# Moving small copies and jump terms of one edge pass from VectorE to ScalarE in a four-layer graph network

## What is computed

```
val = att_self[edge_row] + att_neigh[edge_col]
mx = jax.ops.segment_max(val, edge_row, num_segments=n)
val_exp = jnp.exp(val - mx[edge_row]) * edge_val[:, None]
denom = jnp.clip(jax.ops.segment_sum(val_exp, edge_row, num_segments=n), 1e-10)
msg = val_exp[:, :, None] * h_neigh[edge_col]
agg = jax.ops.segment_sum(msg, edge_row, num_segments=n) / denom[:, :, None]
```

## Time and profile before

| what | value |
|---|---|
| median of the runs | 6677.1 us (6671.12 to 6688.41) |
| span of the profiled execution | 7599.6 us |
| `sorted_pass` in it | about 2970 to 3411 us, 56 groups |
| VectorE busy, whole program | 4666.3 us (61%) |
| GpSimd busy | 4386.9 us (58%) |
| ScalarE busy | 1410.9 us (19%) |
| TensorE matmuls | 1283.1 us (17%) |

### The profile page before, as it was taken

How to read it: one execution, slowest core, us unless ns; L and a number is a source line. 1 busy time by engine, 2 the same in 40 slices (tenths; PEclk the granted TensorE clock), 3 DMA queues, 4 the chain that set the end, 5 groups by cost and what they waited for, 6 DMA issues and landing times. The chain is left out here.

```text
span 7599.6 us, 37104 instructions
## 1 busy us (share of the span) xinstructions
PE 1283.1 (17%) x8049; PEld 1112.1 (15%) x8049; DVE 4666.3 (61%) x9328; ACT 1410.9 (19%) x3648; POOL 4386.9 (58%) x4445
## 2 busy tenths in 40 slices
PE   7100000143443333333000000370000001000000
PEld 6100000033343333332000000250000001000000
DVE  7677777687676667996677777544443434433435
ACT  0122212220000002442000000262222211222223
POOL 1666566545565554005666666426777767777775
PEclk9555555555555555556555555585555555555555
DMA  9555445323333224773555555203333332333332
GB/s 347 179 181 185 164 161 171 120 85 103 101 109 103 95 98 157 296 268 91 176 179 174 180 179 181 85 20 93 106 99 101 101 90 66 111 102 101 97 100 80
DMA packets 338944, 1032.97 MB, mean 136 GB/s; under 512 B 100325, under 2 KB 163137, under 8 KB 331294
## 3 DMA queue, kind: packets, MB, share of 16 engines
q0 software_dynamic: 166752, 401.68, 18.9%
q1 hardware_dynamic: 116642, 342.34, 12.9%
q10 hardware_dynamic: 55324, 286.57, 10.1%
HBM read 602.97 MB, written 427.39 MB: 136 GB/s over the span
## 5 line engine op out<-in xcount | busy, mean ns | idle before, releaser
L708 POOL DMA_INDIRECT rows<-table,idx x3136 | 3091.7, 986 | 1446.0 <-issue 1022.3
L635 POOL DMA_INDIRECT by_src<-ebuf,place x784 | 767.8, 979 | 561.4 <-DVE place L1277 295.9
L1280 DVE SCALAR_TENSOR_TENSOR psA<-psA,cont,dstf 128x128 f32<-128x128 f32 (+1 forms) x2349 | 838.0, 357 | 291.2 <-remote 205.9
L1269 DVE TENSOR_TENSOR sc<-rows,ebuf 128x56 f32<-128x56 f32 x112 | 28.2, 252 | 1196.5 <-DMA rows<-table,idx 1196.5
L1280 DVE SCALAR_TENSOR_TENSOR sums<-sums,cont,psA 128x128 f32<-128x128 f32 (+1 forms) x1512 | 521.2, 345 | 225.0 <-remote 139.9
L934 PE MATMUL psA<-dstf,ones 128*128 128x512 f32 x10 | 9.9, 1113 | 3446.9 <-DVE dstf L2169 3446.9
L803 PE MATMUL psA<-attr,sums 128*128 128x49 f32 x1568 | 406.0, 403 | 747.4 <-DVE attr L1458 735.3
L803 PEld LDWEIGHTS psA<-attr,sums 128*128 128x128 f32 x1568 | 397.0, 326 | 761.1 <-DVE attr L1458 748.7
L934 PEld LDWEIGHTS psA<-dstf,ones 128*128 128x128 f32 x10 | 2.7, 318 | 3448.6 <-issue 3448.6
L2050 DVE TENSOR_TENSOR_SCAN psA<-rows,psA 128x1980 f32<-128x1980 f32 x112 | 480.0, 4286 | 3.9
L1211 ACT ACTIVATE psA<-df 128x60 f32<-128x60 f32 (+1 forms) x168 | 40.4, 241 | 2104.9 <-DVE df L1269 1120.4
(11 more groups left out here) (332 smaller groups left out, 5548.4 us busy)
## 6 DMA issues: line engine op xcount, KB each, us to landing
dstf<-spread_wide SPq DMA_DIRECT2D x168, 924.0 KB
states<-sums ACTq DMA_DIRECT2D x150, 952.0 KB, 3.7
rows<-by_src SPq DMA_DIRECT2D x55, 1035.0 KB, 5.1
states<-sums ACTq DMA_DIRECT2D x56, 1008.0 KB
spread_wide<-sums SPq DMA_DIRECT2D x56, 924.0 KB, 24.3
states<-sums ACTq DMA_DIRECT2D x56, 903.0 KB
rows<-table,idx POOLq DMA_INDIRECT x3136
msg<-low_rows SPq DMA_DIRECT2D x56, 448.0 KB
```

Source lines behind the costliest of these rows:

```text
L635: pool.indirect_dma_start(by_src[:, :], bass.IndirectOffsetOnAxis(ap=place[:, s, j:j + 1], axis=0), payload[:, s, j, :], None).then_inc(so ...
L708: pool.indirect_dma_start(rows[:, at:at + GW[ph]], None, table[ph][:, :], bass.IndirectOffsetOnAxis(ap=idx[:, s, j:j + 1], axis=0)).then_i ...
L1269: return dve.tensor_tensor(o_, a_, b_, op)
L1280: return dve.scalar_tensor_tensor(o_, a_, s_, b_, op0, op1)
```

## The change

The three copies and the jump terms are computed by ScalarE, and three things follow from that in the order of the work.

- ScalarE gets `costs(g + 1)`: jump terms, carried maxima and scores, three ACTIVATEs. In its stream they stand behind the DMA issue of group g - 1 and in front of `scale_tail(g)`. They wait for `flags_ready` and tell `costs_ready`, for which `max_so_far` waits on VectorE.
- ScalarE gets `keep_max(g + 1)`, one ACTIVATE behind `exponentials(g + 1)`, which tells `kept_max`; the DMA that saves the group waits for it.
- On VectorE `chain_flags` runs two groups ahead (so `cg` has three buffers) and stands between rows 10 and 11. `edge_bias(g)` moves from behind row 11 to behind row 9. `messages` waits for `pass_saved`, which `keep_max` did before.
- Before the first group, `chain_flags(1)` follows `chain_flags(0)`, ahead of the first scan.

The change to `holds` alters a count that phases 3 and 4 do not use.

```diff
-        cg = sb("cg", [P, 2, B])
+        cg = sb("cg", [P, 3, B])
...
+                def costs(g):
+
+                    act.wait_ge(flags_ready, g + 1)
+                    act.activation(hb(nf)[:, :, 1:B + 1], cg[:, g % 3, :].unsqueeze(1).to_broadcast([P, 4, B]), ACT.Copy, scale=BIG, bias=-BIG)
+                    act.activation(hb(sc)[:, :, 0], hb(mx)[:, :, B], ACT.Copy)
+                    act.activation(hb(sc)[:, :, 1:B + 1], srows[g % 3][:, 1:B + 1, ROW:ROW + 4].rearrange("p b h -> p h b"), ACT.Copy).then_inc(costs_ready, 1)
+
+                def keep_max(g):
+
+                    if g >= 3:
+                        act.wait_ge(pass_saved[g % 3], 16 * (g // 3))
+                    act.activation(ssums[g % 3].rearrange("p (b w) -> p b w", w=136)[:, :, ROW:ROW + 4].rearrange("p b h -> p h b"),
+                                   hb(mx)[:, :, 1:B + 1], ACT.Copy).then_inc(kept_max, 1)
...
+                costs(0)
                 exponentials(0)
+                keep_max(0)
                 for g in range(NG):
+                    if g < NG - 1:
+                        costs(g + 1)
                     scale_tail(g)
...
                     if g < NG - 1:
                         exponentials(g + 1)
+                        keep_max(g + 1)
+                    act.wait_ge(kept_max, g + 1)
                     act.wait_ge(sums_ready, NG + g + 1)
...
-                def chain_costs(g):
-
-                    fronted()
-                    front(ts(hb(nf)[:, :, 1:B + 1], cg[:, g % 2, :].unsqueeze(1).to_broadcast([P, H, B]), -1.0, ALU.add, BIG, ALU.mult))
...
                 def max_so_far(g):
 
-                    fronted()
+                    dve.wait_ge(costs_ready, g + 1)
...
-                    fronted()
+                    dve.wait_ge(flags_ready, g + 1)
                     dve.wait_ge(weighed, g + 1)
                     dve.wait_ge(sums_ready, NG + g)
+                    if g >= 3:
+                        dve.wait_ge(pass_saved[g % 3], 16 * (g // 3))
...
                 chain_flags(0)
-                chain_costs(0)
-                carry_max(0)
-                scores(0)
+                chain_flags(1)
                 max_so_far(0)
                 max_of_all(0)
                 below_max(0)
-                keep_max(0)
...
                     if g < NG - 1:
-                        chain_flags(g + 1)
-                        add_row(g, 1)
-                        chain_costs(g + 1)
-                        add_row(g, 2)
-                        carry_max(g + 1)
-                        add_row(g, 3)
-                        scores(g + 1)
-                        add_row(g, 4)
+                        for j in range(1, 5):
+                            add_row(g, j)
                         max_so_far(g + 1)
...
                         add_row(g, 9)
-                        keep_max(g + 1)
+                        edge_bias(g)
                         add_row(g, 10)
+                        if g < NG - 2:
+                            chain_flags(g + 2)
                         add_row(g, 11)
-                        edge_bias(g)
                         add_row(g, 12)
```

More of the change, by code:

```diff
@@ L300, in build @@
         gates_ready = sem("gates_ready")
+        flags_ready = sem("flags_ready")
+        costs_ready = sem("costs_ready")
+        kept_max = sem("kept_max")
         states_turned = sem("states_turned")
@@ L1012, in exponentials, with hb @@
                     act.activation(exqs[g % 2], df[:, 0:n], ACT.Exp).then_inc(weights_ready, 1)
+                def hb(ap):
+                    return ap[:, 0:n].rearrange("p (h b) -> p h b", h=4)
+                def costs(g):
[8 more added lines that the diff above has]
+                                   hb(mx)[:, :, 1:B + 1], ACT.Copy).then_inc(kept_max, 1)
                 def scale_tail(g):
@@ L1618, in chain_flags @@
                     if g:
-                        front(tt(cg[:, g % 2, :], R3[:, 1:B + 1, ITEM - 1], R3[:, 0:B, ITEM - 1], ALU.is_equal))
+                        tt(cg[:, g % 3, :], R3[:, 1:B + 1, ITEM - 1], R3[:, 0:B, ITEM - 1], ALU.is_equal).then_inc(flags_ready, 1)
                     else:
                         front(dve.memset(cg[:, 0, 0:1], 0.0))
-                        front(tt(cg[:, 0, 1:B], R3[:, 2:B + 1, ITEM - 1], R3[:, 1:B, ITEM - 1], ALU.is_equal))
-                def chain_costs(g):
-                    fronted()
-                    front(ts(hb(nf)[:, :, 1:B + 1], cg[:, g % 2, :].unsqueeze(1).to_broadcast([P, H, B]), -1.0, ALU.add, BIG, ALU.mult))
[L1629 to L1635, removed]
+                        tt(cg[:, 0, 1:B], R3[:, 2:B + 1, ITEM - 1], R3[:, 1:B, ITEM - 1], ALU.is_equal).then_inc(flags_ready, 1)
                 def max_so_far(g):
-                    fronted()
+                    dve.wait_ge(costs_ready, g + 1)
                     front(dve.tensor_tensor_scan(fm[:, 0:n], nf[:, 0:n], sc[:, 0:n], 0.0, ALU.add, ALU.max))
@@ L1650, in below_max @@
                     tt(df[:, 0:n], sc[:, 0:n], mx[:, 0:n], ALU.subtract).then_inc(scores_ready, 1)
[L1652 to L1657, removed]
                 def weigh(g):
@@ L1686, in add_row @@
                     prev = S3[:, j - 1, 0:F] if j else fixr[:, 0:F]
-                    m = stt(S3[:, j, 0:F], prev, cg[:, g % 2, j:j + 1], psA[:, msg_at[j]:msg_at[j] + F], ALU.mult, ALU.add)
+                    m = stt(S3[:, j, 0:F], prev, cg[:, g % 3, j:j + 1], psA[:, msg_at[j]:msg_at[j] + F], ALU.mult, ALU.add)
                     if j < B - 1:
@@ L2009, in _ @@
                 sr = Steps(scores_ready, NG * ph)
-                holds = Steps(hold_step, (B - 1) * NG * ph)
+                holds = Steps(hold_step, (B - 1) * NG * min(ph, 2))
                 accs = Steps(acc_step, (B - 1) * NG * ph)
```

## The result

The changed kernel takes 6692.1 us (median of 12 runs, 6683.1 to 6698.5) against 6677.2 us (12 runs, 6667.8 to 6688.4) for the kernel before. The ratio is 1.002, 95% interval 1.0012 to 1.0027: slower by 8 to 18 us, 14.9 us between the medians. That is inside the 0.3% called "same" above, on the side forecast, and larger than the 10.0 us forecast.

The account below looks back on a forecast made before the run. VectorE's dependent row chain, bound by the time from a row's start to its semaphore, sets the pace; 8.1 us over 54 groups plus 1.9 us at the start gave 6677.1 + 10.0 = 6687.1 us, eight-in-ten range 6669 to 6704 us.

Parts of the forecast that it names:

- same: Whole kernel: about 0.3%, 20 us, is what a measurement can tell from no change; chance of landing inside 0.78.
- The bound: VectorE's row chain: each step costs 0.388 us with or without a small instruction in its gap; removing four gains 0 us.
- the faster rival: VectorE's chain: the small instructions do cost their place, 26 us in all, giving 6651 us; chance 0.06.
- a small instruction in the gap: Between VectorE's chain rows: jump terms, carried maxima, scores and kept maxima, 0.16 to 0.21 us long, priced at 0 us.
- the ring: Row 13, DMA issue, tail, product, bias add, rows 10 to 13: VectorE waits 0.14 us; period 7.85 against 7.70 us.
- The link from row 13 to the DMA issue: ScalarE's DMA issue waits for row 13; the forecast kept this distance unchanged at 0.37 us.
- The wait in the messages: One wait more ahead of VectorE's messages: 0 us, at most 0.04 x 53 = 2 us.
- The step to row 11: VectorE's chain: this step already has a second wait and takes 0.39 us like the others, so another costs nothing.
- The start: Before the first group: first scan 2.4 us later, as second flags need the second load; 0.54 us taken back, 1.9 us once.
- The sum: Whole kernel: 8.1 us in the groups plus 1.9 us at the start, 10.0 us more, 6687.1 us.
- the ring's term: Steady groups 1 to 54: 0.15 us more per group, 8.1 us in all.

Follow-up runs that it names:

- The shared gap above: Kernel before with the bias add behind row 9, beside the kept maxima: 430.6 us, period 7.79 us; with kept maxima moved behind row 10: 425.6 us, 7.70 us.
- The two experiments that take it apart at either end: Changed kernel with its three ScalarE instructions ahead of the DMA issue: 427.7 us; changed kernel with the bias add back behind row 11: 427.5 us.
- doubling it: Changed kernel with the three ScalarE instructions done twice, first into unused space: 459.4 us, period 8.36 us.
- the one with only its start repaired: Changed kernel with the second group's flags computed ahead of the first weigh: messages 438.2 us, median period 7.94 us.

## Why the prediction was right, and where it was short

*The bound.* Right. The chain is set by the row-to-row latency, and the four moved instructions rode in it free. The comparison in the earlier trace rows carried it: the bare rows of the last group gave 0.388 us, and the bare rows of the changed kernel 0.39 us. The gain of 26 us of the faster rival did not come. The rule of the Trainium skill named beside it (VectorE: DVE Perf Modes, Rules for kernel authors) tells to minimize the operation count in chained VectorE work; here the count fell by four per group and the steps stayed at 0.39 us. The shared gap above shows a case in which one instruction less in a gap does count: 0.10 us.

The prediction took "a small instruction in the gap" as free in general. It read this from instructions of 0.16 to 0.20 us. The longer ones are not quite free, as the section on the hardware shows, but none of them was taken away.

*The mechanism of the loss.* Right: the three instructions ahead of the tail, the product, the bias add, the ring. The two experiments that take it apart at either end gave back 9.3 and 9.5 us, and doubling it cost 22.4 us.

*Its size.* Short by 0.09 us per group: 7.85 us forecast, 7.94 us measured. Two terms were mis-sized. The link from row 13 to the DMA issue was carried over as 0.37 us and is 0.43 us, because `kept_max` had been put ahead of the wait for row 13; I had looked at the additional wait in the messages and not at this one. The three instructions were put at 0.14 + 0.10 + 0.14 = 0.38 us and took 0.16 + 0.10 + 0.19 = 0.44 us (2628.49, 2628.65, 2628.74, 2628.93). The first two lie near; the third, the strided read of scores followed by the first tail instruction, had no like row. The estimate of 376 ns worked out from figures of the Trainium skill (ScalarE: Activation LUTs, under "What ACT_TABLE_LOAD costs") was short in the same way. The other links came out near the forecast: product to bias add 2.06 us, bias add to row 13 1.39 us; together with the tail and the copies they were 0.03 us shorter than summed, so 0.06 + 0.06 - 0.03 = 0.09 us.

*The wait in the messages.* Priced at 0, bound 0.04 us, measured 0.07 us. It did not enter the result, since the ring covered it; without the ring it would cost an estimated 0.07 x 55 = 4 us. The step to row 11, which I took as evidence, has its additional wait behind the one that comes last. The number of waits alone was the wrong question: what counts is how many are taken behind the one that comes last (see the section on the hardware).

*The start.* Forecast were 2.4 us less the 0.5 us that the first group takes back, 1.9 us. Measured were 2.1 us less 0.6 us, 1.5 us. The mechanism was right; the first group's part came back as a loss as soon as the start was repaired.

*The sum.* 13.0 us in the 54 groups and 1.5 us at the start, 14.5 us, where 8.1 + 1.9 = 10.0 us were forecast; the runs gave 14.9 us, interval 8 to 18 us. That the start came out 0.4 us under its forecast hid a little of the 4.9 us by which the ring's term was too small.

## What to carry to other kernels

A small instruction that stands in the gap of a dependent chain can be free where it is (here up to 0.21 us long, one per gap); before moving it, compare a stretch of the chain with and without such fillers. Work moved to an engine with idle time is free only if it is put into that idle time: here the same three instructions cost 9 us behind ScalarE's DMA issue and nothing ahead of it. When a step is moved earlier, ask what its input's slack is at the new place, and add up every link that leads to it, the waits among them. Look at the first group by itself: what is early or late there differs from the steady groups.

## What the runs showed of the hardware

**The order of semaphore waits ahead of an instruction matters.** With the wait that is satisfied last put first, VectorE's messages start 0.38 us behind row 13, with two or with three other waits beside it; put last of three, 0.47 us; third of four, 0.55 us. ScalarE's DMA issue starts 0.37 to 0.38 us behind row 13 with it alone or first, and 0.43 us with it second. The reordered line alone was worth 5.5 us in this pass.

The traces show why. The waits beyond one are semaphore instructions of their own, which the timeline leaves out and a query by source line gives. Around the group shown above, kernel after, where row 13 runs from 2627.68 to 2628.02:

```profile
L1677 DVEq EVENT_SEMAPHORE  x1: 21/21/21, 2628.1 to 2628.1; - x1
L1679 DVEq EVENT_SEMAPHORE  x1: 50/50/50, 2628.1 to 2628.1; - x1
```

And with the wait for row 13 first, where row 13 runs from 3195.40 to 3195.75:

```profile
L1677 DVEq EVENT_SEMAPHORE  x1: 21/21/21, 3195.5 to 3195.5; - x1
L1679 DVEq EVENT_SEMAPHORE  x1: 50/50/50, 3195.6 to 3195.6; - x1
```

In the changed kernel both stand behind the end of row 13 and ahead of the messages. In the other they are done while row 13 still runs, so the wait for row 13 isn't in either of them and they delay nothing. The kernel before has one such instruction per group, the changed kernel two: that is the step from 0.47 us to 0.55 us.

**What fits into a gap of the chain.** With one instruction of 0.16 to 0.21 us between two rows the step is 0.38 to 0.39 us, as bare. A longer one shows even alone: with the bias add (0.27 us) the step is 0.45 us, with the first scan (0.28 us) 0.46 us. With two, 0.21 and 0.27 us long, it is 0.55 us. Timeline of the kernel before, row 4 being at 3207.22:

```profile
3207.49 0.28 DVE L1640 TENSOR_TENSOR_SCAN fm<-nf,sc 128x60 f32<-128x60 f32 x1
...
3207.68 0.71 DVE L1280 SCALAR_TENSOR_TENSOR dstf<-dstf,cg,psA 128x132 f32<-128x132 f32 x2
```

**The sort took longer in one trace, the pass did not.** The sort before the pass took 1300 us in the profiled execution of before and 1016 us in that of after, 284 us of the 907 us between them, with the same busy time on VectorE to 1%. Busy time by stretch, first before, then after:

```profile
1668.00:2968.00 1300.00, 511.27 (x3822) 490.49 (x3822) 906.92 (x1394) 110.61 (x221) 766.85 (x783) 0.50 0.31 100
```
```profile
1456.00:2472.00 1016.00, 506.12 (x3822) 488.85 (x3822) 914.51 (x1393) 109.87 (x220) 769.77 (x783) 0.50 0.40 128
```

The change doesn't touch the sort, and what differs there was not tried. It did not reach this pass, whose period was the same to 0.01 us in executions of 6693.0 us and 7536.9 us (7.94 us for the changed kernel and for the one with only its start repaired), which is why the traces could decide where the medians could not.
